# Two of four query tiles move behind the first scores, the first keys are loaded inside the first stage, and the feed-forward gets two bank sets and its residual by identity passes

## What is computed

```python
x = layernorm(x + self_attention(x))          # 32 heads of 16, causal, linear position bias
x = layernorm(x + cross_attention(x, ctx))    # 32 query heads, 8 key heads of 128, RMS norm of q and k
x = layernorm(x + feed_forward(x))            # columns permuted, 16 groups 32 -> 128 -> gelu -> 32, permuted back
# cross_attention: kv = concat(ctx, x); q = rms(x @ Wq) * w; k = rms(kv @ Wk) * w; v = kv @ Wv
#                  softmax(q k^T / sqrt(128)) v @ Wo
```

## Time and profile before

| | |
|---|---|
| Median of three runs | 885.67 us (884.92 to 885.82) |
| Profiled execution: span, time, mean clock | 881.7 us, 883.53 us, 0.98 |
| PE, PEld, DVE, ACT, POOL busy | 834.4, 698.2, 567.6, 462.6, 505.6 us |
| First block, about | 0 to 287.6 us |
| Second block, about | 287.6 to 840.3 us |
| Third block, about | 840.3 to the end |
| DMA queue q1 | 55.59 MB, 20.0% of 16 engines |

### The profile page before, as it was taken

One profiled execution on the slowest core, in us unless ns is written; L12 is line 12 of the kernel. 1 busy time (PEld: TensorE's weight loads), 2 busy tenths in 40 slices (PEclk: granted clock), 3 DMA queues, 4 the chain that ended last, 5 costly groups with the idle time before them and its releaser, 6 DMA issues. The chain is left out here.

```text
span 881.7 us, 15131 instructions
## 1 busy us (share of the span) xinstructions
PE 834.4 (95%) x4833; PEld 698.2 (79%) x4833; DVE 567.6 (64%) x1538; ACT 462.6 (52%) x981; POOL 505.6 (57%) x655
## 2 busy tenths in 40 slices
PE   7999999899898699999999999999999999999975
PEld 5777776677676688888888888888888888888753
DVE  4377675777542576676677667667667767777535
ACT  5666653555322365555556456555555645556242
POOL 2565863665311786756765775775675676445711
PEclk9999999999999699999999999999999999999978
DMA  6503132121113621121121122122121102000011
GB/s 223 183 26 132 63 100 81 56 64 49 48 48 96 222 67 66 36 67 67 37 65 65 36 65 65 36 65 65 36 65 65 36 12 67 1 1 1 0 25 48
DMA packets 48463, 56.23 MB, mean 64 GB/s; under 512 B 4622, under 2 KB 29724, under 8 KB 48412
## 3 DMA queue, kind: packets, MB, share of 16 engines
q1 hardware_dynamic: 48412, 55.59, 20.0%
HBM read 41.95 MB, written 13.63 MB: 63 GB/s over the span
## 5 line engine op out<-in xcount | busy, mean ns | idle before, releaser
L1090 POOL TENSOR_SCALAR prob<-prob,x_rinv 128x768 f32<-128x768 f32 x128 | 116.2, 908 | 166.8 <-DVE x_rinv L1265 166.8
L1207 ACT ACTIVATE pT_hi<-bank 128x512 fp32r<-128x512 f32 x192 | 114.4, 597 | 96.6 <-PE bank L1422 96.0
L1186 ACT ACTIVATE prob<-bank,x_nm,q_rms 128x768 f32<-128x768 f32 x128 | 127.1, 993 | 49.2 <-DVE x_nm L1259 48.9
L1256 DVE TENSOR_REDUCE x_mx<-bank 128x1 f32<-128x768 f32 x128 | 122.1, 954 | 26.3 <-PE bank L1380 26.2
L1318 DVE TENSOR_TENSOR pT_lo<-bank,pT_hi 128x512 fp32r<-128x512 f32 x192 | 130.4, 680 | 8.5 <-ACT pT_hi L1207 6.9
L1422 PE MATMUL bank<-ident,prob 128*128 128x128 f32 x768 | 116.2, 274 | 5.3 <-POOL prob L1090 5.3
L1422 PEld LDWEIGHTS bank<-ident,prob 128*128 128x128 f32 x768 | 95.8, 141 | 17.6 <-POOL prob L1090 6.4
L398 ACT ACTIVATE s_self<-s_self,nm_self 128x128 f32<-128x128 f32 (+1 forms) x128 | 57.0, 447 | 66.5 <-DVE nm_self L514 66.4
L48 PE MATMUL bank<-pT_hi,xv_hi 128*128 128x512 f32 x192 | 86.6, 451 | 0.9 <-DVE pT_lo L1318 0.8
L50 PE MATMUL bank<-pT_hi,xv_lo 128*128 128x512 f32 x192 | 75.8, 395 | 0.0
L49 PE MATMUL bank<-pT_lo,xv_hi 128*128 128x512 f32 x192 | 75.4, 393 | 0.0
(11 more groups left out here) (196 smaller groups left out, 2042.8 us busy)
## 6 DMA issues: line engine op xcount, KB each, us to landing
wo_raw<-in_Wo SPq DMA_DIRECT2D x8, 1024.0 KB, 5.4
wq_raw<-in_Wq SPq DMA_DIRECT2D x7, 1024.0 KB, 5.5
v_by_head<-v_st SPq DMA_DIRECT2D x12, 512.0 KB, 3.3
kT_by_head<-kT_st SPq DMA_DIRECT2D x12, 512.0 KB, 3.2
xk_raw<-kT_by_head SPq DMA_DIRECT2D x16, 384.0 KB, 3.2
xv_raw<-v_by_head SPq DMA_DIRECT2D x16, 384.0 KB, 3.1
wq_raw<-in_w_attn SPq DMA_DIRECT2D x12, 256.0 KB, 4.4
xk_raw<-in_ctx SPq DMA_DIRECT2D x8, 256.0 KB, 2.5
```

What stands on the lines that cost most here:

```text
L1090: nc.gpsimd.tensor_scalar(prob[:, s, :], prob[:, s, :], rinv[:, s:s + 1], 1.0, ALU.mult, ALU.mult)\
L1186: nc.scalar.activation(prob[:, s, :].rearrange("p (a e) -> p a e", a=2), bank[:, at:at + 2, 0:HALF], ACT.Exp, bias=nm[:, s:s + 1], scale=q ...
L1207: nc.scalar.activation(pT_hi[:, a, :], bank[:, turn.bank[s, what, a], :], ACT.Copy)\
L1256: nc.vector.reduce_max(mx[:, s:s + 1], bank[:, at:at + 2, 0:HALF], AX.XY)\
```

## The change

First block: `Q 2` and `Q 3` leave the list, `Q 0` and `Q 1` come at its end; `W 8` comes after `XT 3` and writes into `wq_hi`, `wq_lo`, which `Y` has then released (`first_wq_*` go); the value groups of row tile 9, `Y`, `LN`, `X1` and `XT` are put in another order. SP loads the first keys ahead of the stores of tile 10, and the waits for all stores stand in the second block's SP stream. Second block: query tiles 2 and 3 are made after the first scores in banks 0 and 3, their mean squares and inverse roots come as a second half, values are loaded before keys, and POOL makes the four norms in a row before the second batch's keys. Third block: up products alternate between banks 0 to 3 and 4 to 7, Gelu's table is loaded by a first tiny activation, x is added by PE (identity times its high and its low part, two passes of 512 columns for each tile, eight in all), scatter passes go by group i over all tiles, DVE reads statistics from PSUM, and ACT writes the normalised rows with scale and bias.

```diff
-        if c == NQ - 2:
-            order.append(("W", 8))
-    parts(q % 2)
-    order += [("PV", NQ // 2 - 1), ("A", NQ // 2 - 1), ("Q", 0), ("Y", 2), ("Y", 3), ("LN", 2)]
-    parts(2)
-    order += [("X1", 2), ("LN", 3), ("Q", 1), ("X1", 3)]
+    order += [("PV", NQ // 2 - 1), ("A", NQ // 2 - 1)]
+    parts(1 + (q + 1) % 2)
+    order += [("Y", 2), ("Y", 3), ("LN", 2)]
+    parts(1)
+    order += [("X1", 2), ("LN", 3)]
+    parts(1)
+    order += [("XT", 2), ("X1", 3)]
     parts(max(0, (B * CT + 2) * PARTS - q))
-    order += [("XT", 2), ("XT", 3)]
-    parts(ROWS * PARTS - 2 - q)
-    order.append(("Q", 2))
-    parts(4)
-    order.append(("Q", 3))
-    parts(3)
+    order += [("XT", 3), ("W", 8)]
+    parts(ROWS * PARTS - q)
+    order.append(("Q", 0))
+    parts(5)
+    order.append(("Q", 1))
...
+                if n == B * CT + LT:
+                    sp.wait_ge(k_store, 16 * n)
+                    sp.wait_ge(bias_made, QUAD * NQ)
+                    sp.wait_ge(ct_ps, B * CT)
+                    sp.dma_start(k.k_raw0[:], k.kT_dram[0, :, 0:KEYS]).then_inc(k.k_in[0], 16)
...
-            sp.wait_ge(v_store, 16 * ROWS)
-            sp.wait_ge(k_store, 16 * ROWS)
-
-            sp.dma_start(k.k_raw0[:], k.kT_dram[0, :, 0:KEYS]).then_inc(k.k_in[0], 16)
...
+            sp.wait_ge(k.v_store, 16 * ROWS)
+            load_values(0, 0)
+            sp.wait_ge(k.k_store, 16 * ROWS)
             load_keys(1, 0)
-            for b in range(B):
-                load_values(b, 0)
+            load_values(1, 0)
...
-            norm(0, 0)
-            keys(1, 0, 0, 2)
-            for j in range(1, UT):
+            for j in range(UT):
                 norm(j, j)
-            keys(1, 1, 0, 3)
+            for p in range(2):
+                keys(1, p, 0, 2 + p)
+            pool.wait_ge(first_ms, 2)
+            nc.gpsimd.tensor_tensor(q_inv[:, columns(1)], q_ms[:, columns(1)], minus_half[:, columns(1)], ALU.pow)\
+                .then_inc(first_inv, 1)
+            pool.wait_ge(first_q_ps, 2)
...
+            for r in range(2):
+                pe.wait_ge(exp_made, r + 1)
+                w = slice((2 + r) * P, (3 + r) * P)
+                for m in range(KT):
+                    last = three_passes(nc, bank[:, FIRST_Q[r], :], k.x1_hi[:, m, w], k.x1_lo[:, m, w],
+                                        wq_hi[:, m, :], wq_lo[:, m, :], m == 0, m == KT - 1)
+                last.then_inc(first_q_ps, 1)
...
+                            if turn.first and s == 0 and a < 2:
+                                pe.wait_ge(first_ss, GRP * (a + 1))
...
+            nc.scalar.activation(warm[:], ident[:, 0:1], ACT.Gelu).then_inc(warm_done, 1)
...
-                    nc.scalar.activation(hid[:, i % 2, r, :], bank[:, r, :], ACT.Gelu).then_inc(h_out, 1)
+                    nc.scalar.activation(hid[:, i, r, :], bank[:, 4 * (i % 2) + r, :], ACT.Gelu).then_inc(h_out, 1)
...
+                nc.scalar.activation(x[:, i, :], bank[:, Z_BANK[i], :], ACT.Identity, bias=shift[:, i:i + 1],
+                                     scale=k.rstd[:, TT + i:TT + i + 1]).then_inc(ln_made, 1)
...
+                elif i == 1:
+                    pe.wait_ge(t_lo, KT)
                 else:
-                    pe.wait_ge(h_out, HPT * i)
+                    pe.wait_ge(h_out, HPT * (i - 1))
+                if i == 3:
+                    pe.wait_ge(y_lo, 1)
...
-                pe.wait_ge(h_out, HPT * (i + 1))
+                pe.wait_ge(h_out, min(HPT * KT, HPT * (i + 1) + (1 if i < 2 else 0)))
...
+                for j in js:
+                    nc.tensor.matmul(bank[:, Z_BANK[j], :], ident_r[:], res_hi[:, j, :], start=True, stop=False)
+                    nc.tensor.matmul(bank[:, Z_BANK[j], :], ident_r[:], res_lo[:, j, :], start=False, stop=False)
...
+            up_products(0)
+            up_products(1)
+            up_products(2)
+            down_products(0)
+            up_products(3)
+            down_products(1)
+            down_products(2)
+            residual((0, 1))
+            scatter_group(0, (0, 1))
+            scatter_group(1, (0, 1))
+            down_products(3)
+            residual((2, 3))
+            scatter_group(0, (2, 3))
+            scatter_group(1, (2, 3))
+            scatter_group(2, range(TT))
+            scatter_group(3, range(TT))
```

More of the change, by code:

```diff
@@ L621, in _ @@
                                             ALU.subtract, ALU.mult).then_inc(x1_made, 1)
-                elif what == "Q" and a < TT - 1:
+                elif what == "Q":
                     dve.wait_ge(q_rows_out, a + 1)
@@ L1197, in _ @@
                 exponentials(j, 0, j, 2 * j)
+            for r in range(2):
+                act.wait_ge(first_q_ps, r + 1)
+                nc.scalar.activation(q[:, 2 + r, :], bank[:, FIRST_Q[r], :], ACT.Copy).then_inc(first_q_out, 1)
             def body(turn):
@@ L1305, in _ @@
                     invert_sum(j - 1, 0, j - 1)
+            for r in range(2):
+                dve.wait_ge(first_q_out, r + 1)
+                for g in range(GRP):
+                    w = slice(g * HD, (g + 1) * HD)
+                    nc.vector.tensor_tensor_reduce(out=q_sq[:, 2 + r, w], in0=bank[:, FIRST_Q[r], w], in1=q[:, 2 + r, w],
+                                                   scale=1.0, scalar=0.0, op0=ALU.mult, op1=ALU.add,
+                                                   accum_out=q_ss[:, (2 + r) * GRP + g:(2 + r) * GRP + g + 1])\
+                        .then_inc(first_ss, 1)
+            dve.wait_ge(first_ss, 2 * GRP)
+            nc.vector.tensor_scalar(q_ms[:, columns(1)], q_ss[:, columns(1)], 1.0 / HD, RMS_EPS, ALU.mult, ALU.add)\
+                .then_inc(first_ms, 1)
             def body(turn):
@@ L1331, in body @@
                                                     f32(oT_hi[:, g:g + 2, rows]), ALU.subtract).then_inc(o_out, 1)
-                    if s == 0 and not turn.first:
+                    if s == 0 and turn.first:
+                        dve.wait_ge(first_inv, 2)
+                        nc.vector.tensor_scalar(q_rms[:, columns(1)], q_inv[:, columns(1)], X_SCALE, None, ALU.mult)\
+                            .then_inc(first_rms, 1)
+                        dve.wait_ge(first_rms, 2)
+                    elif s == 0:
                         query_scales(1, i)
@@ L1538, in _ @@
                 gelus(i)
-                if i > 0:
-                    result_hi(i - 1)
-            result_hi(KT - 1)
+            act.wait_ge(y_ps, KT)
+            nc.scalar.activation(yT_hi[:, KT - 1, :], bank[:, Y_BANK[KT - 1], :], ACT.Copy).then_inc(last_y_hi, 1)
+            for i in range(TT):
+                act.wait_ge(shift_made, i + 1)
+                nc.scalar.activation(x[:, i, :], bank[:, Z_BANK[i], :], ACT.Identity, bias=shift[:, i:i + 1],
+                                     scale=k.rstd[:, TT + i:TT + i + 1]).then_inc(ln_made, 1)
         @block.vector
@@ L1616, in up_products @@
                         q = slice(FD * r, FD * (r + 1))
-                        done = nc.tensor.matmul(bank[:, r, :], weights[q, i, :], rows[q, i, :], start=first, stop=last)
+                        done = nc.tensor.matmul(bank[:, 4 * (i % 2) + r, :], weights[q, i, :], rows[q, i, :], start=first,
+                                                stop=last)
                         if last:
@@ L1634, in _ @@
                     permute(i, b)
-            for i in range(KT):
-                up_products(i)
-                if i > 0:
-                    down_products(i - 1)
-            down_products(KT - 1)
-            for j in range(TT):
-                w = slice(j * P, (j + 1) * P)
-                for i in range(KT):
-                    if j == 0:
-                        pe.wait_ge(y_lo, i + 1)
-                    nc.tensor.matmul(bank[:, j, :], yT_hi[:, i, w], scatter[:, i, :], start=i == 0, stop=False)
-                    last = nc.tensor.matmul(bank[:, j, :], yT_lo[:, i, w], scatter[:, i, :], start=False,
-                                            stop=i == KT - 1)
-                last.then_inc(z_ps, 1)
+            up_products(0)
[14 more added lines that the diff above has]
+            scatter_group(3, range(TT))
 class Kept:
```

109 lines of the change are left out of this document (66 added, 43 removed).

## The result

The changed kernel takes 878.95 us (median of 4 runs, 877.83 to 879.79) against 885.29 us (median of 4, 883.60 to 885.82) of the kernel before on the same chip: ratio 0.9936, 95% interval 0.9915 to 0.9956, so 3.9 to 7.5 us less. Forecast were 878.5 us and a range of 874.5 to 882.5. The total was met. The three parts, read from the profiled executions, were not all met: the first block gave 2.8 us less than forecast.

A forecast was written before the change was run, and what follows sets the result against it. PE was taken to bound the long middle, so gains and losses at the edges count whole. Both boundaries net -4.35 us and feed-forward -2.9 sum to -7.2, applied to the 885.67 us median: 878.5 us, range 874.5 to 882.5.

The forecast's parts named there:

- First block: Sum of the first block's terms up to the second block's begin: cross-attention begins 8.4 us earlier.
- The query tiles: First block: two of four query tiles leave it, 2.8 us each, so 5.6 us less.
- the stall behind the Wq split: First block: PE's 2.02 us wait behind DVE's split of the first Wq goes, 2.0 us less.
- the boundary: Between first and second block: keys load ahead of tile 10's stores, gap 2.15 us instead of 5.1, so 3.0 less.
- the wait for normalised tile 3: First block, x's split transposes: PE goes on 2.95 us after the first begins instead of 2.1, 0.85 us more.
- +1.4 behind `v_st`: First block: third group of row tile 10 waits for DVE's copy, there at 7.6 instead of 6.2, 1.4 us more.
- +2.05 for POOL: Second block's start: POOL waits for query sums, last norm of the second unit at 32.65 us instead of 30.6.
- +2.0 for the low clock behind the wait: Second block: half speed for about 4 us after PE's wait at the second unit's transposes; bounds 0 and 3.1 us.
- Feed-forward: Third block: early table load, two bank sets, addition on PE, lighter DVE tail; end at 876.4, 2.9 us less.
- Rival 1: Second block: the wait does not lower the clock and scores run high; gain kept, -11.5 us, 874.2 us, chance 0.2.
- Rival 2: Third block: low clock in the idle pieces between Gelus, feed-forward pays nothing; -4.35 us, 881.3 us, chance 0.2.
- Rivals 3 and 4: Second block, low clock through scores into query tiles: all given back, 885.4 us, chance 0.07; or slower, 888.5 us, chance 0.05.

The follow-up runs named there:

- four_q: The changed kernel with all four query tiles in the first block, none in the second; 885.98 us, ratio 1.0015 to the kernel before.
- late_keys: The changed kernel with the first keys' load and the waits for all stores back at the first block's end; 881.14 us, ratio 0.9960.
- list_order: The changed kernel with the first block's list reordered: third value group of row tile 9 ahead of the second statistics, normalised tile 3 earlier; 875.15 us.
- pool_order: The changed kernel with POOL's first-turn norms of unit 1 made between the next Wq's weight pieces instead of behind them; 874.65 us, ratio 0.9880.
- filled_hole: The changed kernel with unread identity transposes filling PE's waits at the second unit's transposes in the first turn; 876.55 us, ratio 0.9911.
- ff_only: The kernel before with only its feed-forward replaced by the changed one, first and second blocks old; 882.15 us, ratio 0.9967.
- blocks_only: The changed kernel's first and second blocks with the feed-forward of the kernel before; 880.34 us, ratio 0.9952.
- early_q: The changed kernel with first-block list and POOL queue reordered, plus query tile 2 before the first scores and a keys piece between POOL's norms; 866.50 us.
- last: early_q with unit 0's four norms in a row again and row tile 10's first key group ahead of x's fourth transpose; 867.30 us, ratio 0.9796.

## Why the prediction was right in sum, and where it was wrong

- **First block, forecast -8.4, measured -5.6.** This is the same in all five traces of this first block in which the clock fell once (59.91 to 59.96 us, for 65.52 and 65.53 before). The query tiles (`four_q`: 5.4 for 5.6), the stall behind the Wq split and the boundary (1.93 us left where 2.15 were forecast, and `late_keys` gives 2.65 of the forecast 3.0) came as worked out. So did the wait for normalised tile 3: the first part of row tile 10 begins 2.87 us after the third transpose, 2.95 forecast. The step that failed is the one on the new order of `Y`, `LN` and the value groups. I followed tile 3 and `W 8` through it, and not the ring of banks 5 and 6: `Y 3` takes the bank of parts (9, 4) and (9, 5), whose copy stands on DVE behind `LN 2`, which waits for `Y 2`. That is the 2.63 us, and `list_order` removes them.
- **The +1.4 behind `v_st`** was not seen as a wait. PE came later to that place, because its clock was low from 246.7 to 250 after the two earlier waits; low clock took the place of the wait at about the same price (some 1.7 us for 1.4).
- **Second block, +2.05 for POOL, measured 1.24** between the two first traces, and 2.0 between the means of seven traces and of two. That POOL sets the second unit's start was right (`pool_order`). The forecast called POOL's new wait the cost, and that was wrong: POOL waits 0.22 us for the sums (the forecast's own figures, 17.6 and 17.95, had 0.35), and without them nothing is got back (`four_q`). What the term holds in fact is the second inverse root, 1.64 forecast and 1.65 measured. In the profiled execution scores ended 9.74 us after the begin instead of 10.5, which took 0.8 off.
- **+2.0 for the low clock behind the wait, measured 2.7** in the profiled execution, within the forecast's bounds of 0 and 3.1, and 2.1 in the mean of six kernels, later norms included (`filled_hole`). I had it last 4 us; the windows show 0.50 from 312 to 318. The other 0.84 us of the +4.76 are the stall at 423.59, which no term could have had.
- **Feed-forward, -2.9, measured -3.0** where the clock at the block's begin is alike (`ff_only`), -1.8 in the two traces. Both prices behind it held: 1.1 us for the addition on DVE, and 1.0 for the table load, which the forecast took from its row (1.28) and not from the 2.66 of the Trainium skill.
- **The sum.** Measured terms give -5.6 + 4.8 - 3.0 = -3.8 us, at the edge of the 3.9 to 7.5 that the times say; with the means over all traces in the second block (556.45 us in six, 552.24 in two, so +4.2 for the forecast's +4.05) they give -4.4. The forecast of -7.2 was 2.8 us too good in the first block, and met the median (-6.3) because that holds some 2 us which the traces do not show. So the total was met in part by luck. The two traces of old blocks come from executions that were 2.1 and 4.4 us faster than their medians, so they may understate what the old kernel loses; that the missing 2 us lie in the clock is likely, given the spread of `blocks_only`, but it was not shown.
- **The signs** that were named: block 2 at 280.61 for 279.3; POOL's first weight piece 18.9 us after the begin for 19.6; the second unit's transposes waiting 2.6 us for 3, with the clock at 0.50 behind them; the first Gelu 0.3 us after its scores for 0.2; DVE's last statistics at 873.60, 2.05 us before SP's last store is issued (875.65), for 2.3. None of the signs of being wrong showed: the boundary gap was 1.93 us, and PE had no wait in the scatter passes. The one that pointed to a missed step was the begin of block 2, and with the 1.4 us of the run's start it was late by 2.7.
- **Rivals.** Rival 1 (no clock loss) did not happen: the clock was 0.50 behind the wait. `pool_order` reached nearly its time (874.65 for 874.2), but by taking the wait away. Rival 2 (low clock in the feed-forward's pieces of idle) did not happen in any trace of the new feed-forward; in the changed kernel PE's windows from 846 to its last pass are at 1.00. Rivals 3 and 4 needed the low level through the query tiles; the clock was 0.58 from 286 to 288 and 1.00 from 288 on, two tiles of scores ahead of them.

## What to carry to other kernels

When a hand-written order moves an instruction, follow for each engine what is queued behind it, and for each bank who uses it next: both losses of this change were a finished result standing in its reader's queue, once behind an instruction that had to wait (the copy behind `LN 2`), once behind work that was wanted later (the norms behind the weight pieces). Taking them away by two reorderings and filling one more wait gave 11 to 12 us on top of the change's 6, without one matmul less. And price a wait of the bounding engine with the clock behind it: here waits that put the second unit back by 1.2 to 2.0 us came with some 1 to 3 us of low clock, and meaningless transposes in the wait won 2.7 us back. And look along the whole trace before a difference of two stretches is given to a cause: 0.84 us of one came from a single slow instruction 100 us further on.

## What the runs showed of the hardware

- The same idle stretch is not always followed by the low clock. 2.52 us of idle PE at the first transposes in `early_q` left it at 1.00, 1.83 us at the same place in `last` brought it down, and ahead of the third block, always 3.2 us, the level fell at different points, so that work up to the up products took 11.0 or 12.2 us. The Trainium skill's page "TensorE: Matmul & The Clock Gate", section "What's actually happening", says that the chip's look at PE's activity runs freely and is not reset when a kernel starts. The rows agree with that: the same wait met the fall at another point from one execution to the next.
- Single transposes of a 128 x 128 identity, 18 in 2.13 us, and 6 and 5 in the two shorter waits, stood where PE had waited for POOL, and the clock was 1.00 through and behind them (`filled_hole`, one trace).
- The same DVE instruction (`q_ms`, 128 x 8) took 1.30 us in three of 14 traces, at the same place of the program, and 0.17 to 0.20 in the others; the trace shows no reason. PE was 0.84 us later behind it each time.
- ACT's pass with a scale and a bias from SBUF, out of PSUM, takes 0.78 us for 128 x 512 (871.50 and 872.63 in the changed kernel), where a plain copy takes 0.60.
